# Two expert layers: the second bias of each block comes by its own broadcast DMA and is added as the rows leave PSUM, instead of by gate transposes and gate-bias matmuls

## What is computed

```python
# layer e0: inner width 1024, one expert per token
for e in range(8):
    h = gelu(x @ w1[e] + b1[e])
    y = h @ w2[e] + b2[e]
    out = out + where(expert_idx == e, expert_w, 0)[:, None] * y
# layer e2: inner width 512, the two best experts, gates that add up to 1
out = einsum('besh,ehd->besd', gelu(x @ W1 + b1), W2) + b2
y = einsum('bse,besd->bsd', gates, out)
```

## Time and profile before

| what | value |
|---|---|
| time, median of 3 runs | 1867.71 us (1862.19 to 1872.19) |
| profiled execution: span from first to last instruction | 1836.7 us |
| its own time outside the span | not recorded; the median of the runs is 31.0 us above the span |
| TensorE busy | 1603.0 us, 87% of the span |
| VectorE, ScalarE, GpSimd busy | 58%, 49%, 21% |
| granted TensorE clock, mean | 0.945 of full |
| blocks of e0 | about 293 to 477 us of the span |
| blocks of e2 | about 1494 to 1664 us of the span |

### The profile page before, as it was taken

How to read it: one execution, slowest core, us unless ns; L and a number is a source line. 1 busy time by engine, 2 the same in 40 slices (tenths; PEclk the granted TensorE clock), 3 DMA queues, 4 the chain that set the end, 5 groups by cost and what they waited for, 6 DMA issues and landing times.

```text
span 1836.7 us, 27973 instructions
## 1 busy us (share of the span) xinstructions
PE 1603.0 (87%) x9998; PEld 1210.8 (66%) x9998; DVE 1070.4 (58%) x3023; ACT 906.0 (49%) x2034; POOL 379.8 (21%) x480
## 2 busy tenths in 40 slices
PE   6999959999679999999858799999998779995566
PEld 5677638889557666676535567777665468894444
DVE  7767752222456676666567665555555535325887
ACT  4888821222146666666549355555554102233366
POOL 1000014111232333323240100000001332223734
PEclk9999989999789999999979899999999889997878
DMA  9000028888400000000000200000000438893001
GB/s 342 2 1 1 2 92 325 292 290 288 143 7 6 7 7 7 7 1 1 1 1 1 81 12 7 7 7 7 1 1 12 135 132 264 300 354 120 0 12 35
DMA packets 61625, 151.99 MB, mean 83 GB/s; under 512 B 9216, under 2 KB 39696, under 8 KB 55248
## 3 DMA queue, kind: packets, MB, share of 16 engines
q1 hardware_dynamic: 54096, 133.65, 22.1%
q0 software_dynamic: 5280, 14.47, 2.1%
q10 hardware_dynamic: 2112, 2.10, 0.4%
HBM read 133.63 MB, written 24.75 MB: 86 GB/s over the span
## 4 chain that ended last, share of the span: by engine, by line
PE 69%; DVE 15%; ACT 6%; POOL 4%; issue 4%; DMA 1%; POOLq 1%; SPq 0%; DVEq 0%; ACTq 0%
PE bank L1036 8%; PE bank L979 8%; PE bank L1459 8%; PE bank L1513 7%; PE bank L1526 6%; PE bank L1500 5%; PE bank L1463 5%; PE bank L1443 3%; PE bank L679 3%; POOL sorted_h L1224 2%; PE bank L695 2%; PE bank L1865 2%; PE bank L710 1%; ACT p1f L1581 1%; PE bank L616 1%
## 5 line engine op out<-in xcount | busy, mean ns | idle before, releaser
L1710 DVE TENSOR_REDUCE small<-bank 128x1 f32<-128x512 f32 x128 | 82.5, 686 | 108.8 <-PE bank L1513 108.8
L1055 ACT ACTIVATE e2a<-bank,WB 128x128 f32<-128x128 f32 x156 | 44.5, 368 | 178.6 <-PE bank L1036 178.6
L1706 DVE CUSTOM_DVE_ANT_0 p1f<-bank,p1f 128x512 f32<-128x512 f32 x128 | 83.2, 687 | 81.0 <-PE bank L1513 81.0
L1584 ACT ACTIVATE p2f<-bank,small 128x512 f32<-128x512 f32 x128 | 86.8, 683 | 86.2 <-DVE small L1710 86.2
L751 ACT ACTIVATE l<-l,small 128x256 f32<-128x256 f32 x256 | 108.9, 502 | 32.6 <-DVE small L817 32.2
L1581 ACT ACTIVATE p1f<-p1f,small 128x512 f32<-128x512 f32 x128 | 91.2, 713 | 67.5 <-DVE small L1706 67.2
L400 POOL TENSOR_SCALAR rs<-mv 128x4 f32<-128x4 f32 x16 | 3.6, 226 | 566.8 <-DVEq L230 551.1
L817 DVE CUSTOM_DVE_ANT_0 l<-bank,small 128x256 f32<-128x256 f32 x256 | 90.8, 420 | 13.4 <-PE bank L695 12.5
L1459 PE MATMUL bank<-WA,HT 128*128 128x256 f32 x384 | 93.4, 387 | 5.0 <-DVE p1f L1651 5.0
L1595 ACT ACTIVATE p2f<-bank 128x512 f32<-128x512 f32 x128 | 75.1, 598 | 40.6 <-PE bank L1500 39.1
L1055 ACT ACTIVATE e0a<-bank,WB 128x128 f32<-128x128 f32 x128 | 36.5, 367 | 106.2 <-PE bank L1036 106.2
(11 more groups left out here) (401 smaller groups left out, 3939.1 us busy)
## 6 DMA issues: line engine op xcount, KB each, us to landing
WB<-in_L2pack SPq DMA_DIRECT2D x39, 514.0 KB, 5.3
WB<-in_L2pack SPq DMA_DIRECT2D x39, 512.0 KB, 5.5
WB<-in_L0pack SPq DMA_DIRECT2D x16, 1028.0 KB, 6.4
WB<-in_L0pack SPq DMA_DIRECT2D x16, 1024.0 KB, 7.3
e0a<-in_L0pack SPq DMA_DIRECT2D x7, 1028.0 KB, 7.1
e0a<-in_L0pack SPq DMA_DIRECT2D x7, 1024.0 KB, 6.8
sorted_h<-in_blank SPq DMA_DIRECT2D x6, 1032.0 KB, 16.2
e2a<-sorted_h SPq DMA_DIRECT2D x39, 129.0 KB, 5.3
```

The lines of the kernel that those rows point to most:

```text
L1584: ins = a.e.activation(P, k.bank(x), ACT.Exp, bias=self.mx[:, m:m + 1], accum_out=self.sm[:, m:m + 1])
```

## The change

- The gate tiles `G` and `GT`, the rows `b2` in SBUF, their load and the tests `biased` go: with them 16 transposes, 16 copies, 16 bias products and 16 additions to `X` in each layer, and the semaphore value `GATED` that TensorE waited for.
- `load_down` issues a second DMA behind the down weights, for every block: the expert's row of `b2` (1 KB in DRAM), broadcast to the 128 partitions of one of `nwb` new buffers `yb`. Before it, SyncE waits until VectorE has taken the rows of the block that last used this buffer (`yc`).
- Both DMAs count on the same semaphore `a2`, and `down_pe` waits for both.
- VectorE's copy of `y` becomes an addition: PSUM + `yb`. The bias then gets its gate in `finish`, as the rest of the row does.

The diff, without the lines that only remove names:

```diff
@@ __init__
-        self.L, self.G, self.E = (r(128, t=16, e=8) for _ in range(3))
+        self.L, self.E = (r(128, t=16, e=8) for _ in range(2))
...
-        self.b2 = r(256)
+        self.yb = [r(256) for _ in range(nwb)]
...
-        self.a2 = [k.dma(f"gather{4 + i}", len(range(i, nt, nwb))) for i in range(nwb)]
+        self.a2 = [k.dma(f"gather{4 + i}", 2 * len(range(i, nt, nwb))) for i in range(nwb)]
@@ pe
-        t.wait_ge(self.a_b2, 1)
-        t.wait_ge(self.routing, self.GATED)
@@ down_pe
         t.wait_ge(self.yc, i - 1)
-        if self.biased(i) is not None:
-            t.e.matmul(y[:, 256:512], self.GT[i % 3][0:8, :], self.b2[0:8, :], start=True, stop=True)
-        t.wait_ge(self.a2[i % self.nwb], i // self.nwb + 1)
+        t.wait_ge(self.a2[i % self.nwb], 2 * (i // self.nwb + 1))
@@ turn_pe
-        t.wait_ge(self.routing, self.GATED)
-        if self.biased(i) is not None:
-            t.e.transpose(T[0:8, 256:384], self.G[:, self.biased(i), :], k.ident[:, :])
@@ worth
-            v.chain(e.tensor_tensor(S[:, 0, :, :], S[:, 0, :, :], S[:, 1, :, :], ALU.add))
-            e.tensor_tensor(G, S[:, 0, :, :], bc(d), ALU.mult).then_inc(self.routing.sem, 1)
-        else:
-            e.tensor_copy(G, S[:, 0, :, :]).then_inc(self.routing.sem, 1)
@@ dv
-            if self.biased(i) is not None:
-                k.residual(v, self.biased(i), k.bank(4 + i % 2)[:, 256:512], None)
-            v.e.tensor_copy(self.ys[i % 3], k.bank(4 + i % 2)[:, 0:256]).then_inc(self.yc.sem, 1)
+            v.e.tensor_tensor(self.ys[i % 3], k.bank(4 + i % 2)[:, 0:256], self.yb[i % self.nwb], ALU.add).then_inc(self.yc.sem, 1)
@@ turn_dv
-        if self.biased(i) is not None:
-            v.e.tensor_copy(self.GT[i % 3][0:8, :], k.bank(6 + i % 2)[0:8, 256:384])
@@ load_down
         s.e.dma_start(w[:, self.n1:n].rearrange("p (o n) -> p o n", o=1),
                       self.pack[bass.ds(x, 1), :, self.n1:n].rearrange("o p n -> p o n")).then_inc(self.a2[i % self.nwb].sem, 16)
+        s.wait_ge(self.yc, i - self.nwb + 1)
+        s.e.dma_start(self.yb[i % self.nwb], self.b2d[bass.ds(x, 1), :].to_broadcast([128, 256])).then_inc(self.a2[i % self.nwb].sem, 16)
@@ sp
-        s.e.dma_start(self.b2[0:8, :], self.b2d).then_inc(self.a_b2.sem, 16)
```

More of the change, by code:

```diff
@@ L847 @@
 class Experts:
-    SHIFTED, SELECTED, PLACED, KNOWN, GATED = 1, 2, 3, 4, 5
+    SHIFTED, SELECTED, PLACED, KNOWN = 1, 2, 3, 4
     def __init__(self, k, tag, heir, ff, topk, nt, temp, bias, nwb):
@@ L883, in __init__ @@
         self.ys, self.first_gelu = [r(256) for _ in range(3)], r(1)
-        self.GT = [r(128) for _ in range(3)]
         io = k.io
@@ L890, in __init__ @@
         self.cleared = (k.setup.z0, 3) if tag == "e0" else (k.setup.z2, 5)
-        self.a_b2 = k.dma("b2", 1)
         late = 3 if topk == 1 else 0
@@ L908, in __init__ @@
             self.seated, self.place_of = f("p_cxn", 4), r(4, i=2, n=2)
-        self.routing = f("e_routing", 5)
+        self.routing = f("e_routing", 4)
         self.xt_t, self.xt_d = f("e_xt_t", nt), f("e_xt_d", nt)
@@ L981, in down_pe @@
         ins.then_inc(self.dn.sem, 1)
-    def biased(self, i):
-        return i - 2 if 2 <= i < 18 else None
     def logits_pe(self, t, g):
@@ L1085, in worth @@
     def worth(self, v):
-        e, G, E, M, S = v.e, self.G, self.E, self.M, self.S
+        e, E, M, S = v.e, self.E, self.M, self.S
         topk, d, gv, bc = self.topk, self.d, self.gv, self.over
```

## The result

| | before | after |
|---|---|---|
| time, median of 4 runs each | 1869.26 us (1862.19 to 1872.19) | 1840.61 us (1834.91 to 1842.47) |
| ratio, 95% interval | | 0.9853 (0.9832 to 0.9875) |
| TensorE busy in the profiled execution | 1603.0 us | 1583.6 us |

The kernel is faster by 28.7 us, or 1.5%. The time of 1841 that stood in the prediction is met to half a microsecond. The steps behind it did less well: in e2 the bias loads cost two to three times what was put down for them, and that the total is met so closely is luck.

The account below looks back on a forecast made before the run. TensorE was taken to set the pace of both block loops, with the DMA engines nearly as slow. -14.7 (e0) - 14.7 (e2) + 2 = -27.4, say -27 us: span near 1810, time 1841, range 1833 to 1858.

Parts of the forecast that it names:

- TensorE's part, 14.7 + 14.7: Block loops of e0 and e2: 0.92 us less TensorE work in 16 blocks each, 14.7 us per layer, 29.4 together.
- I take 2 us for e2: Layer e2's block loop: the added bias loads on the DMA engines cost 2 us of the gain.
- about 5 us: Layer e2: weights arrive before they are wanted, leaving about 5 us of slack with the bias load behind them.
- idle time of TensorE before the down product: Layer e2, line 973: idle time ended by a DMA would show the 2 us loss was a wrong step.
- The price of a broadcast: DMA engines: one 128 KB bias load takes 0.41 us of all engines, at 0.050 us a packet.
- about 375 GB/s, 3.85 us: Layer e2: rate the DMA engines can give, and the resulting time per block with the bias load.
- The 6 us of loss: Layer e2: by the skill's 358 GB/s rule a block takes 4.04 us and the loss is 6 us instead of 2.
- "Nothing" in e0: Layer e0: the bias loads cost 0, since up loads have slack 9 us and TensorE stays the pace.
- SyncE's queue, VectorE, the dropped wait for the gates: Both layers: SyncE's issues stay under 3.73 us a block, VectorE's changes and the dropped wait bring nothing or 0.03 us.
- The DMA engines become the bound in e2: Rival, layer e2: blocks take 4.01 to 4.14 us, loss 5 to 10, gain 19 to 24, time 1843 to 1849; chance 0.2.
- The broadcast loads are slow in themselves: Rival, both layers: reading one 1 KB row 128 times is slow; gain gone at 0.82 us a load; chance 0.05.
- The same 31.0 is put on top: Whole kernel: the median of runs stands 31.0 us above the profile's span, added again to the predicted span.

Follow-up runs that it names:

- before again: The kernel before, unchanged, profiled a second time on the first chip: 1863.27 us, span 1861.5.
- a_third: The changed kernel, unchanged, run again on the third chip: 1818.03 us against 1842.9 for the kernel before, ratio 0.9867.
- e6_distinct_rows: Changed kernel; in layer e2 each bias load is followed by an unread load of 128 different 1 KB rows: 1826.48 us, ratio 0.9918 against the kernel before.
- e3_double: Changed kernel with each bias row of layer e2 loaded twice, the second copy unread: 1869.32 us, ratio 1.015 against the kernel before.
- e1: Changed kernel without bias loads, the wait for `yc` and the addition, in both layers: 1836.17 us, ratio 0.9845 against the kernel before.
- e2_deep: Changed kernel with 16 bias buffers instead of 4 in layer e2, so SyncE's wait is always met: 1816.66 us, ratio 0.9851 against the kernel before.

## Why the prediction was right

**TensorE's part, 14.7 + 14.7.** Right to half a microsecond in each: 15.2 us in e0 and, without the one slow block of before again, 15.2 in e2. The mechanism is the predicted one, blocks of 7.24 us throughout in e0 and of 3.73 in e2 wherever no DMA is late.

**"I take 2 us for e2."** This is the step that failed. The loads cost 5.0 us on the first chip, and 3.9 to 6.2 over five profiles. The term that was too large is the slack of "about 5 us", which was worked out for the weights alone. The rows of a block were what TensorE waited for; they go out 7.5 us ahead of their use and land after 5.5 to 7.0, and that leaves 0.5 to 2 us. With the throughput that was measured, (361 + 372) / 2 = 367 GB/s, a block takes 1.445 MB / 367 = 3.94 us; by the prediction's own formula 36 x (3.94 - 3.73) less a slack of 1.3 is 6.3, less 5 it is 2.6. The sign that was named for this failure, idle time of TensorE before the down product, did not come; it came before the transposes. The price of a broadcast was too low as well: 0.050 us a packet from the earlier trace rows, whose packets read 1 KB each of their own, against 64 to 73 ns for the broadcast's packets in e2 (47 in e0, with one load in 7.24 us). The net gain in e2 was 15.2 less 3.9 to 6.2, so 9 to 11, against 12.7; the 12.0 on the first chip contains before again's slow block.

**"about 375 GB/s, 3.85 us".** The engines gave 361 and 372 GB/s in after, 365 in `a_third`, 369 in `e6_distinct_rows`, over 40 us each. I had it nearly right, and for the reason given: the 360 of before's last blocks was what TensorE asked for, not all there is. The Trainium skill's figure of about 358 GB/s for a core's share of HBM ("DMA: Bandwidth & Descriptors", section "Where 436 GB/s comes from") was passed for 40 us at a time with one core busy. The 6 us of loss estimated from it is nearer to the 5.0 measured than my 2, but it has the same slack of 5 in it, and the rate it rests on is not the one at which this core stopped: `e6_distinct_rows` moved 369 GB/s, and `e3_double` stood at 263 with the engines as full.

**"Nothing" in e0.** Right: TensorE is busy for all of 340 to 440 us, and the 1 us by which `e1` is shorter is the granted clock at the loop's start.

**SyncE's queue, VectorE, the dropped wait for the gates.** As predicted: nothing of theirs shows. `e2_deep` took the new wait away and gained nothing. VectorE's addition takes 425 ns.

**The rivals.** *The DMA engines become the bound in e2* came in part: share 1.02 and 1.03, and a loss at or near its lower end of 5 us. It is nearer to what happened in e2 than the forecast's "2 us". *The broadcast loads are slow in themselves* had a mechanism that is real; with one load a block all that the loads cost was 3.9 to 6.2 us and not the 29.4 that it needed, with two it was 52.3 more. (By its own formula the gain is gone at 0.81 us a load and the kernel 9.3 us slower at 0.98, where 0.82 and 0.99 stand.) The Trainium skill's rule on a leading zero-stride broadcast (same page, "Rules for kernel authors") sets no limit for 128 copies, and the landing agrees with that: 6.6 us in the median, where one engine alone would need about 128 x 0.070 = 9.0, an estimate from the packets' 70 ns.

**"The same 31.0 is put on top".** Wrong in its meaning. Time and span differ by 1.8 us; the rest of the 31.0 most likely stood for another chip. It did no harm because the gain was worked out as a difference, and the gains of the two loops together are the same on both kinds of chip to a microsecond or two.

**Why the total still fitted.** Predicted gain 27; measured by the medians 28.7 on the first pair and 24.9 (1842.9 to 1818.03) on the third chip; by the loops 15.2 in e0 and 9 to 11 in e2, so 24 to 26.5. The forecast was 1 to 3 us too high by the loops: 2 to 4 us too little for the loads, against 1 us too little for TensorE. The medians of the same two kernels scatter by as much as that, and the 0.5 us between forecast and result is luck.

## What to carry to other kernels

A small product that stands on the path of the busiest engine can be worth removing even where the DMA engines are nearly full: here a tenth more bytes a block gave back a third of the gain in e2 and nothing in e0. Work out the loss from the slack of *every* load that the engine waits for, the smallest included, from its issue and its use in the trace. Price a broadcast from DRAM by a row that reads one address many times, not by one that reads as many bytes, and where several would be under way at once, load the rows once and pick by register.

Before a profile's span is set against a median of runs, look whether its own time belongs to them; where it doesn't, compare loops, not spans.

## What the runs showed of the hardware

- The same 128 KB cost 0.30 us of e2 a block when it came from 128 rows and 1.34 when it came from one row that was already read by another load. Packets of 1 KB took 47 ns on average at one broadcast per 7.24 us, 64 to 73 at one per 3.8 to 4, 119 at two per 5.4; half of them took 46 ns in each case, and the rest made the difference.
- The DMA share counts packets under way: 1.02 at 263 GB/s, 1.03 at 369.
- Chips differ by 26 us on the same kernel (1868.89 on one, 1843.16 and 1842.9 on two others). About 20 of them lie in the burst ahead of e2's first block, where SyncE took 22 to 24 us to issue four loads that took 3.8 elsewhere. About 4 more lie ahead of e0's first up product, which comes 5.1 us after the start of the last product before it (line 959) in before again (6.0 in after), and 1.1 us after it in the first profile of before and in `a_third`. What makes them was not found: the one experiment on it ran on a chip that doesn't show them.
